# Who makes minus the mean and variance plus epsilon: the vector engine or GpSimd, in the two layer norms of a transformer block

## The reference

```
n  = (x - mean(x)) / sqrt(var(x) + 1e-5)
x  = x + proj(softmax(q k^T / 4) v) + proj_b        # q, k, v = n @ qkv_w^T + qkv_b
m  = (x - mean(x)) / sqrt(var(x) + 1e-5)
x  = x + fp8(clip(m / s_in, -448, 448)) * s_in @ w + bias
```

## Time and profile before

| | us |
|---|---|
| median of 3 timed runs (lowest, highest) | 1055.44 (1053.39, 1057.67) |
| the profiled execution | 1050.12 |
| its span | 1048.3 |
| busy in the span: PE / DVE / ACT / POOL | 945.9 / 843.0 / 655.7 / 522.7 |

### The profile page before, as it was taken

The page is one execution under the profiler, slowest core; times in us unless marked ns, Lnnn a source line. Parts: engine busy times, 40 slices in busy tenths (PEclk is TensorE's granted clock), DMA queues, the critical chain, the costliest instruction groups (busy, mean ns, idle before and its releaser), DMA issues.

```text
span 1048.3 us, 16257 instructions
## 1 busy us (share of the span) xinstructions
PE 945.9 (90%) x5796; PEld 443.0 (42%) x5796; DVE 843.0 (80%) x1186; ACT 655.7 (63%) x1209; POOL 522.7 (50%) x533
## 2 busy tenths in 40 slices
PE   3476989999999999999999999999999999999884
PEld 2243334444444434454444444444444444433333
DVE  3586788888888989888888889888888888896226
ACT  3013776767676676767676676767676776766560
POOL 3141344828284654728293755638282846524242
PEclk9675999999999999999999999999999999999795
DMA  4928092656638192746648291836556380911010
GB/s 138 116 44 94 26 119 41 97 88 77 108 45 139 21 115 51 108 77 82 103 56 129 30 117 39 119 66 92 93 68 96 40 125 14 117 35 42 2 41 20
DMA packets 44289, 79.40 MB, mean 76 GB/s; under 512 B 9904, under 2 KB 13104, under 8 KB 44208
## 3 DMA queue, kind: packets, MB, share of 16 engines
q1 hardware_dynamic: 44208, 78.36, 50.5%
HBM read 18.42 MB, written 8.39 MB: 26 GB/s over the span
## 4 chain that ended last, share of the span: by engine, by line
PE 81%; ACT 6%; POOL 4%; DVE 3%; issue 2%; DMA 2%; SPq 1%; ACTq 0%; POOLq 0%; DVEq 0%
PE ps_t L457 28%; PE ps_o L489 23%; PE ps_m L371 9%; PE ps_s L471 5%; ACT pt L568 5%; PE ps_m L382 5%; PE ps_m L408 5%; PE ps_m L439 3%; POOL xnT_p L907 2%; SPq L282 1%; ACT xnT L587 1%; POOL xnT_p L905 1%; DVE mx L686 1%; DMA ks<-parts 1%; PE ps_m L355 1%
## 5 line engine op out<-in xcount | busy, mean ns | idle before, releaser
L568 ACT ACTIVATE pt<-ps_t 128x512 f32<-128x512 f32 x1024 | 557.5, 599 | 242.5 <-PE ps_t L457 238.0
L686 DVE TENSOR_REDUCE mx<-ps_s 128x2 f32<-128x1024 f32 x512 | 617.6, 1213 | 93.3 <-PE ps_s L471 87.9
L457 PE MATMUL ps_t<-qs,ks 50*128 50x512 f32 x1024 | 406.9, 467 | 41.1 <-ACT pt L568 34.7
L471 PE MATMUL ps_s<-ks,qs 48*128 48x512 f32 x1024 | 399.8, 472 | 20.0 <-DMA ks<-parts 11.4
L457 PEld LDWEIGHTS ps_t<-qs,ks 50*128 50x128 f32 x1024 | 164.7, 187 | 360.2 <-ACT pt L568 288.4
L489 PE MATMUL ps_o<-pt,vt 128*32 128x512 f32 x2048 | 275.3, 610 | 0.2 <-ACT pt L568 0.2
L471 PEld LDWEIGHTS ps_s<-ks,qs 48*128 48x128 f32 x1024 | 160.1, 189 | 31.3 <-DVE mx L686 16.1
L905 POOL CAST xnT_p<-xnT 128x512 fp32r<-128x512 f32 x30 | 18.3, 611 | 195.2 <-ACT xnT L587 195.2
L371 PE MATMUL ps_m<-xnT_p,wqkv_p 128*128 128x512 f32 x360 | 101.1, 417 | 7.6 <-POOL xnT_p L907 7.6
L939 POOL TENSOR_TENSOR on<-ot,rden 128x256 f32<-128x256 f32 x63 | 39.6, 628 | 103.8 <-DVE rden L745 103.8
L930 POOL TENSOR_TENSOR parts<-parts 128x512 f32<-128x512 f32 x60 | 81.2, 1353 | 4.9
(11 more groups left out here) (94 smaller groups left out, 766.4 us busy)
## 6 DMA issues: line engine op xcount, KB each, us to landing
qs<-parts SPq DMA_DIRECT2D x192, 128.0 KB, 6.5
ks<-parts SPq DMA_DIRECT2D x192, 128.0 KB, 7.0
xin<-in_x SPq DMA_DIRECT2D x16, 512.0 KB, 4.6
xres<-in_x SPq DMA_DIRECT2D x16, 512.0 KB, 5.9
out<-h SPq DMA_DIRECT2D x15, 512.0 KB, 9.0
qs<-nmax SPq DMA_DIRECT2D x128, 8.0 KB, 5.7
pt<-in_qkv_wT SPq DMA_DIRECT2D x1, 768.0 KB, 6.5
out<-h SPq DMA_DIRECT2D x2, 256.0 KB, 2.0
```

The costliest lines, as they stand in the source:

```text
L457: nc.tensor.matmul(ps_t[:, g, :], ks[par][rows, slot, keys], qs[par][rows, slot, :], start=True, stop=True).then_inc(st_done, 1)
L471: done = nc.tensor.matmul(ps_s[:, s % 2, g, :], qs[par][rows, slot, queries], ks[par][rows, slot, :], start=True, stop=True)
L568: nc.scalar.activation(pt[n % 2][:, w % 2 + 2 * a, w // 2, :], ps_t[:, a, :], ACT.Exp, scale=SCALE).then_inc(exp_done, 1)
L686: dve.tensor_reduce(mx[:, t, :, s % (STEPS // 2)], ps_s[:, s % 2, :, :], AX_X, ALU.max).then_inc(max_done, 1)
```

## The change

DVE no longer makes `nm` and `ve`; it signals after the last `bn_aggr`. POOL itself adds epsilon to the variance (one instruction on 128 x 4 elements, read with a step of two out of `mv`), waits for its own semaphore, takes the power in place, and subtracts the mean straight out of `mv` in the four large instructions (`subtract`, `mult` in place of `add`, `mult`). In `finish` the same is done for each half, and DVE's large instructions there subtract too. The first norm's core:

```diff
                 for j in range(NJ):
                     last = dve.bn_aggr(mv1[:, j, :], st1[:, j, :])
-                last.then_inc(ln1_mv, 1)
-                dve.wait_ge(ln1_mv, b + 1)
-                dve.tensor_scalar(nm1[:], mv1[:, :, 0], -1.0, None, ALU.mult).then_inc(ln1_ready, 1)
-                dve.tensor_scalar(ve1[:], mv1[:, :, 1], EPS, None, ALU.add).then_inc(ln1_ready, 1)
+                last.then_inc(ln1_ready, 1)
...
             def layernorm_x(b, par):
-                pool.wait_ge(ln1_ready, 2 * b + 2)
-                pool.tensor_tensor(rs1[:], ve1[:], half_neg[:], ALU.pow).then_inc(rs1_ready, 1)
+                pool.wait_ge(ln1_ready, b + 1)
+                pool.tensor_scalar(rs1[:], mv1[:, :, 1], EPS, 0.0, ALU.add, ALU.add).then_inc(ve1_ready, 1)
+                pool.wait_ge(ve1_ready, b + 1)
+                settled()
+                pool.tensor_tensor(rs1[:], rs1[:], half_neg[:], ALU.pow).then_inc(rs1_ready, 1)
...
-                    last = pool.tensor_scalar(xn[:, j, :], xin[par][:, j, :], nm1[:, j:j + 1], rs1[:, j:j + 1],
-                                              ALU.add, ALU.mult)
+                    last = pool.tensor_scalar(xn[:, j, :], xin[par][:, j, :], mv1[:, j, 0:1], rs1[:, j:j + 1],
+                                              ALU.subtract, ALU.mult)
```

The second norm has the same edit (`mv2`, `ve2_ready`, `rs2`), and `finish` has it for each half:

```diff
-                    pool.wait_ge(ln2_ready, 2 * b + 2 * half + 2)
-                    pool.tensor_tensor(rs2[:, tok], ve2[:, tok], half_neg[:, tok], ALU.pow).then_inc(rs2_pow, 1)
+                    pool.wait_ge(ln2_ready, b + half + 1)
+                    pool.tensor_scalar(rs2[:, tok], mv2[:, tok, 1], EPS, 0.0, ALU.add, ALU.add).then_inc(ve2_ready, 1)
+                    pool.wait_ge(ve2_ready, b + half + 1)
+                    pool.tensor_tensor(rs2[:, tok], rs2[:, tok], half_neg[:, tok], ALU.pow).then_inc(rs2_pow, 1)
```

More of the change, by code:

```diff
@@ L94, in block_kernel @@
         mv1 = sb("mv1", [P, NJ, 2])
-        nm1 = sb("nm1", [P, NJ])
-        ve1 = sb("ve1", [P, NJ])
         rs1 = sb("rs1", [P, NJ])
@@ L119, in block_kernel @@
         mv2 = sb("mv2", [P, NJ, 2])
-        nm2 = sb("nm2", [P, NJ])
-        ve2 = sb("ve2", [P, NJ])
         rs2 = sb("rs2", [P, NJ])
@@ L179, in block_kernel @@
         ln1_sums = sem("ln1_sums")
-        ln1_mv = sem("ln1_mv")
         ln1_ready = sem("ln1_ready")
         ln2_sums = sem("ln2_sums")
-        ln2_mv = sem("ln2_mv")
         ln2_ready = sem("ln2_ready")
@@ L194, in block_kernel @@
         y_ready = sem("y_ready")
+        ve1_ready = sem("ve1_ready")
+        ve2_ready = sem("ve2_ready")
         rs1_ready = sem("rs1_ready")
@@ L717, in ln2_finish @@
                     last = dve.bn_aggr(mv2[:, j, :], st2[:, j, :])
[L718 to L721, removed]
+                last.then_inc(ln2_ready, 1)
             def split_max(b, t):
@@ L857, in finish @@
                     for j in range(2 * half, 2 * half + 2):
-                        last = dve.tensor_scalar(hn[:, j, :], h[:, j, :], nm2[:, j:j + 1], rs2[:, j:j + 1],
-                                                 ALU.add, ALU.mult)
+                        last = dve.tensor_scalar(hn[:, j, :], h[:, j, :], mv2[:, j, 0:1], rs2[:, j:j + 1],
+                                                 ALU.subtract, ALU.mult)
                     last.then_inc(hn_ready, 1)
@@ L942, in layernorm_h @@
             def layernorm_h(b):
-                pool.wait_ge(ln2_ready, 2 * b + 2)
-                pool.tensor_tensor(rs2[:], ve2[:], half_neg[:], ALU.pow).then_inc(rs2_pow, 1)
+                pool.wait_ge(ln2_ready, b + 1)
+                pool.tensor_scalar(rs2[:], mv2[:, :, 1], EPS, 0.0, ALU.add, ALU.add).then_inc(ve2_ready, 1)
+                pool.wait_ge(ve2_ready, b + 1)
+                settled()
+                pool.tensor_tensor(rs2[:], rs2[:], half_neg[:], ALU.pow).then_inc(rs2_pow, 1)
                 pool.wait_ge(rs2_pow, b + 1)
@@ L951, in layernorm_h @@
                 for j in range(NJ):
-                    last = pool.tensor_scalar(hn[:, j, :], h[:, j, :], nm2[:, j:j + 1], rs2[:, j:j + 1],
-                                              ALU.add, ALU.mult)
+                    last = pool.tensor_scalar(hn[:, j, :], h[:, j, :], mv2[:, j, 0:1], rs2[:, j:j + 1],
+                                              ALU.subtract, ALU.mult)
                 last.then_inc(hn_ready, 1)
```

## The result

The changed kernel takes 1069.84 us in the median of 5 runs (1066.65 to 1078.21), against 1053.39 of the kernel before beside it. The ratio is 1.0175, with a 95% interval of 1.0143 to 1.0208: slower by some 18 us, where 1055.7 was forecast and no difference. The time lies beyond the range, and it is rival B that came about.

What follows compares the result with a forecast made beforehand. PE was taken to bound the kernel (busy 56.43 of 58.33 us in a full slot). Terms 0 + 0 + 0.2 + 0 = +0.2 us took the median 1055.44 to 1055.7; likeliest 1052.5 to 1058.5, 8 in 10 1052 to 1060.

Steps and rivals of the forecast that it cites:

- rival B: Second norm's clip over 2.1 us late for DVE, and DVE for PE: 1061, up to 1074; chance 0.08.
- Subtract in place of add in the large instructions: POOL's four large instructions, 0.54 us each: no difference, bounds -1.1 to +2.0 us for four.
- The threshold of 2.1 us: Second norm in full slots: the clip can come 2.1 us later (0.27 + 0.28 + 1.56) before PE waits.
- The epsilon: POOL's added small instruction and semaphore wait in a full slot: 0.47 us, bounds 0 and 1.5.
- DVE's relief: DVE spared at most some 13 us; in full slots it hides behind PE, taken as zero.
- The first norm in a full slot: POOL waits 3.84 us behind it for DVE, which covers the added 0.47: zero.
- The start: First norm on the chain: 0.25 us goes, 0.47 comes, so +0.2, bounds -0.25 and +1.25.
- SP's cover of 1.24: SP's copies behind the second norm's splits have 1.24 us before SP's next issue, covering the 0.47 delay.
- The end: In `finish` DVE's chain loses 0.24 us, POOL's bias starts 0.2 later: zero, bounds -1.2 and +0.5.

Runs made afterwards that it cites:

- ratio 1.0000 with add: The changed kernel with DVE negating the mean in place in `mv` and the large instructions adding it, epsilon still on POOL: 1051.04 us, ratio 1.0000.
- POOL does all, with add: The changed kernel with POOL itself making minus the mean and adding it in both norms, `finish` as in the change: 1054.65 us, ratio 1.0019.
- the first norm alone: The kernel before with the change in the first norm only (subtract, epsilon on POOL): 1050.65 us, ratio 0.9992.
- subtract alone: The kernel before with DVE copying the mean into `nm` and the large instructions subtracting it, epsilon still on DVE: 1065.49 us, ratio 1.0119.
- the move alone: The kernel before with DVE's `power_of_two` two steps later and its rounding constant one later, norms untouched: 1056.64 us, ratio 1.0002.

## Why the prediction was wrong, point by point

- **The step that failed** is *Subtract in place of add in the large instructions*: "I take no difference". Four of them cost +2.68 us in place of 0. Even the upper bound of +2.0 was too low: it was the longest `tensor_scalar` shown on POOL, a clip with 1.04 on 1024 elements, and a subtract on 256 takes 1.22. The bound took another operation's time for a limit of the engine.
- **What it costs** went as rival B had it: place (the wait of `power_of_two` at the head of DVE's queue), direction and engines. Its price was too low because the same 1.04 stood in it: 2.5 us late there, 3.13 measured. Its higher end, 1074, had 3.5 late.
- **The threshold of 2.1 us** (0.27 + 0.28 + 1.56) was a sum of rows, and it measured as 1.8 to 1.9. `power_of_two` itself accounts for the difference, with 1.08 in place of 0.84: a late one starts beside POOL's cast, which the earlier trace rows had shown. The sum counted its 0.2 in words and left it out of the threshold. 2.11 - 0.24 = 1.87, and 3.13 - 1.87 = 1.26 is what the scores of step 22 are late by (1.25).
- **The epsilon** was right: 0.43 in place of 0.47, and free in the full slots (ratio 1.0000 with add).
- **DVE's relief** was right, it is worth nothing in the median (POOL does all, with add: 1.0019). DVE's busy time fell by 6.7 and not by 12: L757 and L763, now always late, take 2.7 and 4.0 us more in all.
- **The first norm in a full slot** was right in its result: even four subtracting instructions there, +2.7, hide behind POOL's wait of 3.84; with the first norm alone the full slots keep their length.
- **The start** was mis-sized by the same term: +3.0 in place of +0.2. Of that the four subtracting instructions have 2.5, with 6.88 in the changed kernel's first norm in place of 4.35. It shows in the timeline and is lost in the spread of the medians.
- **SP's cover of 1.24** The earlier trace rows was right, and decides once DVE's wait is moved away: in the change the norm is late by 3.1 and the row loads by 20.3 - 18.4 = 1.9, which is 3.1 - 1.24.
- **The end** was right as far as these rows tell: DVE's product on the first half took 1.63 beside POOL's bias (1.64 before), on the second 0.69 (0.70).
- **Chances.** Rival B had 0.08, because "nothing in the rows tells add from subtract". Nothing told that they are alike in a `tensor_scalar` either: none of POOL's before had a subtract. It had `tensor_tensor` with either, alike at 2.39 on 128 x 1024 (L968 adds, L972 subtracts), and that doesn't carry over. An operation that replaces another in 124 instructions on an engine's critical stretch is an unknown with a price, not a zero.

## What to carry to other kernels

An operation that no row shows is to be priced as unknown for each engine and each kind of instruction, even if it looks like its neighbour: here the same `subtract` is free on DVE (401 ns on 128 x 256 in the changed kernel's `finish` and 407 in *subtract alone*, 408 with add) and costs 2.2 times an add on GpSimd. Let the engine that has time negate a few elements, and add in the large instructions. A delay on an engine off the path is free up to a margin that can be read from three timelines, and beyond it is paid in full, in every slot; moving the wait away helped here only as far as the next queue's cover.

## What the runs showed of the hardware that was not expected

- GpSimd's `tensor_scalar` with a subtract: 1.22 us on 128 x 256 and 3.79 on 128 x 1024, against 0.55 to 0.59 and 1.20 with add. The Trainium skill, page "GPSIMD Engine Reference", section "4.1 Engine selection", calls GpSimd roughly line-rate with one input, in a row on elementwise add, mul and max. The rows are near that with add, 0.54 on 128 x 256 against 0.41 on DVE, and not with subtract, which the row doesn't name and which costs 2.5 ns an element more.
- DVE's `power_of_two` took 0.68 where POOL stood idle beside it, and 1.08 where it started 0.08 behind POOL's cast. In the kernel with the move alone, and above in the change (487.20, 487.28):

```profile
478.90 0.62 POOL L939 TENSOR_TENSOR on<-ot,rden 128x256 f32<-128x256 f32 x1
...
479.62 0.68 DVE L767 TENSOR_SCALAR xres<-hn 128x1024 uint32<-128x1024 uint32 x1
482.32 2.39 POOL L968 TENSOR_TENSOR hn<-hn,xres 128x1024 f32<-128x1024 f32 x1 [2.80 <-DVE xres L773]
```

  The Trainium skill, page "SBUF — State Buffer", section "Who interferes with whom", names `tensor_scalar` among the operations that can enter a two-port mode on DVE, in which it and GpSimd exclude each other for a whole instruction. The rows are in line with that: L757 started inside the cast and ended 0.55 after it did. Which mode it ran in, no row shows.
- Waits of PE of 0.51, 0.93 and 0.59 us in one execution were each followed by some 7 us at the lower clock, which cost more than the waits: slots of 61.3 to 61.9 us. Waits of 0.28, 0.48, 0.56 and 0.61 in the same execution were not.
